# The gated sum of the expert results in the edge pass: 16 multiply-adds, or one product and three additions

## The chip, the cores and the metric

The kernel runs on one core of one Trainium2 chip. It is one program over five engines: TensorE (PE, with PEld for its weight loads), VectorE (DVE), ScalarE (ACT), GpSimd (POOL) and SyncE (SP). The metric is the time of one execution in microseconds on the device; of three runs the median is given. What a measurement of this kernel can tell from no change is about 0.2%, some 6 us.

## The reference, cut to what matters

Four layers run one after the other on 128 graphs of 128 nodes with 128 features each: a graph attention, a mixture of 8 experts, a second graph attention, and last a layer that gates 4 experts by an attention over 524288 edges. Only the last is touched:

```
h = x @ W_gat                                   # 16 columns: 4 heads x 4 experts
e = leaky_relu(a_src[src] + a_dst[dst]);  alpha = softmax of e over the edges of a node
agg = segment_sum(h[src] * alpha, dst) + b_gat
scores = layernorm(agg).reshape(M, 4, 4).mean(1)          # one score for each expert
topk_s, topk_i = top_k(scores, 2);  w = softmax(topk_s)
for ei in range(4):
    g = where(topk_i == ei, w, 0).sum(-1)                 # gate of expert ei, 0 for two of the four
    out = out + g * (gelu(x @ W1[ei] + b1[ei]) @ W2[ei] + b2[ei])
return x + out
```

The change is in the last sum: the gates times the results of the four experts, added to x.

## The kernel before

The first three layers and a sort of the edges by target fill the first part of the span. The edge pass (`edges_and_experts1`) is the rest. It has 32 turns, each for a unit of 4 graphs (`UNIT`), so for 4 x 128 nodes; x lies in SBUF as 128 nodes x 128 graphs x 128 features in float32 for the whole kernel. Each engine runs its own loop over the turns, and the order within an engine is the order of the code. No scheduler moves anything. The engines meet only at semaphores.

Turns are counted from 0 here. Turns 0 to 30 are of the first loop (L1495), turn 31 of the second (L1497). GpSimd's gathers of an iteration stand ahead of the window reads of the same turn, so gathers go on beside VectorE's turns 0 to 29, and none are left in turns 30 and 31.

GpSimd, per loop turn (L1532 to L1539): 16 gathers into buffer 0, a wait for buffer 1 (`rows_out[1]`), 16 gathers into buffer 1, a wait for buffer 0 and for `win_free`, and two window reads (`windows`, L1524). A gather (L1518) fetches 128 rows of the node table by the 128 indices in a column of `edge_ids`. So GpSimd issues 34 indirect transfers per turn. SyncE (L1558 to L1571) writes each filled buffer to the edge table; for the second it first waits for `win_seen`, which VectorE gives at the start of its turn (L1389).

VectorE, per turn (`turn`, L1371): it waits for the windows (`win_in`), scores and hides the edges (L1391 to L1410), gives the scores to ScalarE for the exponential (`scored`, `exped`), multiplies the messages (L1417) and sums them (L1426), updates the running sums, normalises (L1437 to L1452), and ranks the experts (L1456 to L1468), with one exponential on ScalarE between (`gap_s` at L1460, `gap_exped` at L1464). The gates are the tile `one`, called gates in the rows, 128 x 4 graphs x 4 experts. Then it waits for TensorE's results (`res_mm`, L1470), which stand in four banks of PSUM (`b_res`, expert by expert, 4 graphs x 128 features each), and combines them (L1474 to L1482), called the combine below. It ends with `summed` (ScalarE then sends y to memory), `res_free` (TensorE may write the results of the next unit), and with three loads of planned numbers into registers before the next turn (L1496).

TensorE, per turn (`turn`, L1637): four transposes, 8 products of 512 columns with ScalarE's Gelu behind each, then for each expert one product that sets the bias (L1650) and 8 of 128 columns (L1653). ScalarE makes the input of the transposes for the next unit only when it has done `gap_s` of this one, so TensorE starts the next unit behind L1460 of this turn and ends it some time in the next turn.

The order around the combine is written out by hand. `step` lets an instruction raise the counter `step_s`; `settle` waits until all of them have; `then` is both. The combine is 16 `scalar_tensor_tensor` of 128 elements per partition, four for each expert, one for each graph, since the gate of a node is one number per partition, graph and expert:

```
to = b_res[:, e, v, :] * one[:, v, e:e + 1] + so_far
```

`so_far` is x for the first expert and `weighed` (SBUF) after it; the last four write y, and a `settle` stands between the experts. Each has one operand in PSUM and one in SBUF.

Of the kernel before, what the change touches and what calls it, by code (L numbers as in the profile page):

```python
# [6 lines left out]
ALU = mybir.AluOpType  # L7
# [7 lines left out]
P = 128  # L15
# [37 lines left out]
UNIT = 4  # L53
# [12 lines left out]
HC1 = HIDDEN1 // P  # L66
# [1095 lines left out]
def edges_and_experts1(nc, sem, a, x, rstd, shift, node, found, counted, source_ids, row_id, table_dram, edges_dram, out, ident, ones):  # L1162
# [5 lines left out]
    E = TOP_EXPERTS  # L1168
    SPAN = UNIT * NODES
    ROOT_GUESS = float(0x5F3759DF)  # L1170
    with ExitStack() as ctx:
        def sb(name, shape, dt=F32):
            return ctx.enter_context(nc.sbuf_tensor(name, shape, dt))

        def ps(name, shape):
            return ctx.enter_context(nc.psum_tensor(name, shape, F32))
# [25 lines left out]
        s4, one, rank, w_taken = (sb(n, [P, UNIT, E]) for n in ("s4", "gates", "rank", "w_taken"))  # L1202
# [3 lines left out]
        w1, b1 = sb("x1_w1", [P, E, HIDDEN1]), sb("x1_b1", [P, E * HC1])  # L1206
        w2, b2 = sb("x1_w2", [P, E * HC1, FEAT]), sb("x1_b2", [P, E, FEAT])
        feat, featT = sb("x1_feat", [P, UNIT, FEAT]), sb("x1_featT", [P, SPAN])
        hid, weighed, y = sb("x1_hid", [P, E * HC1, SPAN]), sb("x1_weighed", [P, UNIT, FEAT]), sb("x1_y", [P, UNIT, FEAT])

        b_next, b_featT, b_hid, b_res = ps("b_next", [P, 512]), ps("x1_b_featT", [P, UNIT, P]), ps("x1_b_hid", [P, 2, SPAN]), ps("x1_b_res", [P, E, UNIT, FEAT])
        b_most, b_due, b_plan = b_featT[:, 0, :], b_hid[:, 0, 0:UNITS], b_res[:, 0, :, :]
# [8 lines left out]
        normed, turned, featT_s, hid_mm, hid_s, hid_free, res_mm, res_free, summed, out_done = (sem(f"x1_{n}") for n in (  # L1221
            "normed", "turned", "featT", "hid_mm", "hid", "hid_free", "res_mm", "res_free", "summed", "out_done"))
# [18 lines left out]
        def take(engine, semaphore, count):  # L1241
            engine.wait_ge(semaphore, count)
            engine.sem_inc(semaphore, -count)  # L1243
# [4 lines left out]
        def _(dve):  # L1248
# [76 lines left out]
            to = node[:, :, ROW:TAB]  # L1325
# [45 lines left out]
            def turn(came, unit, theirs, after):  # L1371
                mine, pair, after = bass.ds(unit * UNIT, UNIT), bass.ds(unit * PAIRS, PAIRS), bass.ds(after * PAIRS, PAIRS)
# [4 lines left out]
                def step(ins):  # L1377
                    ins.then_inc(step_s, 1)
                    done[0] += 1

                def settle():
                    dve.wait_ge(step_s, done[0])

                def then(ins):
                    step(ins)
                    settle()
# [84 lines left out]
                dve.sem_inc(hid_free, 1)  # L1471

                settle()
                for e in range(E):  # L1474
                    if e == E - 1:
                        take(dve, out_done, 16)
                    for v in range(UNIT):
                        so_far = x[:, bass.ds(unit * UNIT + v, 1), :].rearrange("p o f -> p (o f)") if e == 0 else weighed[:, v, :]
                        to = y[:, v, :] if e == E - 1 else weighed[:, v, :]
                        last = dve.scalar_tensor_tensor(to, b_res[:, e, v, :], one[:, v, e:e + 1], so_far, ALU.mult, ALU.add)  # L1480
                        step(last)
                    settle()  # L1482
                dve.sem_inc(summed, 1)
                dve.sem_inc(res_free, 1)
                take(dve, step_s, done[0])
# [9 lines left out]
            with dve.Fori(0, more) as t:  # L1495
                turn(lambda: dve.wait_ge(win_in, (t + 1) * (16 * PAIRS)), planned_unit(dve, t + 1), planned_left(dve, t + 1), planned_unit(dve, t + 2))  # L1496
            with dve.Fori(0, late) as m:  # L1497
                unit = (m + UNITS - rest) & (UNITS - 1)
                turn(late_came, unit, unit, (m + UNITS + 1 - rest) & (UNITS - 1))
# [165 lines left out]
def build(nc, a, out):  # L1665
# [6 lines left out]
    with ExitStack() as top:  # L1672
# [33 lines left out]
        with ExitStack() as ctx:  # L1706
# [48 lines left out]
            def _(dve):  # L1755
# [25 lines left out]
              keys_dram, slots_dram, rows_dram, edges_dram, ids_dram, table_dram)  # L1781
        renew_semaphores()
        edges_and_experts1(nc, sem, a, x, rstd, shift, tab, found, counted[:, :], ids_dram, row_id[:, :], table_dram, edges_dram, out, ident[:, :], ones)


# [52 lines left out]
```

## Time and profile before

| What | us |
|---|---|
| Median of 3 runs | 3113.96 |
| Lowest and highest of the 3 | 3112.32, 3117.3 |
| Span of the profiled execution | 3601.8 |
| Profiled span less the median | 487.8 |
| VectorE busy in it | 2257.8 |
| TensorE busy | 1935.1 |
| GpSimd busy | 1857.5 |
| ScalarE busy | 1215.1 |

The profiled execution is one execution taken by the hardware profiler; its own time is shown by the span from the first to the last instruction, and nothing else of it is listed. The times of the runs are without the profiler. Here the two are far apart, by 487.8 us, so durations of single instructions can be read from the profile, while the sum of its waits isn't that of a timed run. The shares of busy time are means over stages: the edge pass is about the last 1715 us of the span, and turn 0 starts at 1887.1.

### The profile page before, as it was taken

What the parts mean: (1) busy time and instruction counts of PE and PEld (TensorE: products, weight loads), DVE (VectorE), ACT (ScalarE), POOL (GpSimd) and SP (SyncE); (2) the same over time, 40 slices, a digit from 0 to 9 for tenths busy, and PEclk for the clock granted to TensorE, in tenths of its full rate; (3) what the DMA queues carried; (4) which work ended last, traced back from release to release, by engine and by line L of the source; (5) the groups of instructions that cost most, each with busy time, mean ns of one, the idle gap of its engine ahead of it and who ended that gap; (6) DMA issues with size and microseconds to landing.
All of it is one profiled execution on the core that took longest, in us unless ns stands there. A gap on an engine that the chain in (4) does not pass through costs nothing. (4 is left out here: it accounts for less than half of the span.)

```text
span 3601.8 us, 31245 instructions
## 1 busy us (share of the span) xinstructions
PE 1935.1 (54%) x8829; PEld 1316.8 (37%) x8829; DVE 2257.8 (63%) x4422; ACT 1215.1 (34%) x2447; POOL 1857.5 (52%) x1723
## 2 busy tenths in 40 slices
PE   1776642387878645567432455454544444454555
PEld 1555542255655434456311222232222222222223
DVE  8999886989999965554223454454553444544547
ACT  2676754244444323455311122122212122121222
POOL 5400248554544444445575656655655656656561
PEclk9998865699999867777555676676776677767768
DMA  5792001011111121101111111111111111111111
GB/s 198 250 391 84 16 23 39 24 40 37 46 44 41 36 60 40 56 20 23 42 27 23 32 33 32 32 28 38 32 33 32 32 28 31 38 28 32 37 29 30
DMA packets 170130, 192.35 MB, mean 53 GB/s; under 512 B 59241, under 2 KB 126096, under 8 KB 169008
## 3 DMA queue, kind: packets, MB, share of 16 engines
q1 hardware_dynamic: 107616, 118.69, 9.9%
q0 software_dynamic: 57088, 62.48, 8.4%
q10 hardware_dynamic: 5328, 9.97, 0.7%
q8 instruction: 49, 0.80, 0.1%
q14 instruction: 49, 0.40, 0.0%
HBM read 91.70 MB, written 105.25 MB: 55 GB/s over the span
## 5 line engine op out<-in xcount | busy, mean ns | idle before, releaser
L1518 POOL DMA_INDIRECT edge_rows<-node_table,edge_ids x1024 | 1006.5, 983 | 646.2 <-POOLq L1243 345.9
L1646 PE MATMUL x_b_hid<-x_featT,x_w 128*128 128x512 f32 x512 | 362.3, 854 | 281.4 <-PEq L1243 93.5
L1146 POOL DMA_INDIRECT token_results<-arena,token_of x160 | 251.1, 1569 | 294.3 <-ACT arena L1082 216.9
L583 DVE TENSOR_TENSOR sort_ping<-sort_pong 128x1024 f32<-128x1024 f32 (+1 forms) x232 | 395.1, 1744 | 11.3 <-issue 3.8
L1158 POOL DMA_INDIRECT arena<-keys,row_ids x256 | 249.3, 974 | 288.6 <-DVE counts L821 181.0
L583 DVE TENSOR_TENSOR sort_pong<-sort_ping 128x1024 f32<-128x1024 f32 (+1 forms) x230 | 389.9, 1736 | 8.7 <-ACT sort_ping L1016 3.7
L1139 POOL DMA_INDIRECT slots<-arena,send x128 | 177.8, 1389 | 371.9 <-ACT arena L1038 336.9
L1640 PE MATMUL x_b_featT<-ident,x_feat 128*128 128x128 f32 x128 | 34.8, 428 | 581.0 <-issue 385.3
L1653 PEld LDWEIGHTS x_b_res<-x_w,x_hid 128*128 128x128 f32 x2048 | 276.1, 216 | 152.1 <-issue 152.1
L1653 PE MATMUL x_b_res<-x_w,x_hid 128*128 128x128 f32 x2048 | 303.9, 307 | 39.8 <-issue 39.8
L1646 PEld LDWEIGHTS x_b_hid<-x_featT,x_w 128*128 128x128 f32 x512 | 118.9, 262 | 500.2 <-issue 300.9
L1600 ACT ACTIVATE x_hid<-x_b_hid,x_b 128x512 f32<-128x512 f32 x256 | 174.8, 687 | 294.9 <-DMA keys<-sort_pong 129.3
L90 ACT ACTIVATE arena<-x,shift,rstd 128x128 f32<-128x128 f32 x512 | 210.1, 486 | 98.8 <-DMA slots<-arena,send 87.5
L1640 PEld LDWEIGHTS x_b_featT<-ident,x_feat 128*128 128x128 f32 x128 | 22.9, 217 | 587.7 <-issue 587.7
L1607 ACT ACTIVATE w_taken<-w_taken 128x16 f32<-128x16 f32 x32 | 6.9, 216 | 586.5 <-ACTq L1243 357.3
L252 PE MATMUL banks<-arena 128*128 128x129 f32 x512 | 96.4, 347 | 183.3 <-DVE x L279 94.3
L1480 DVE SCALAR_TENSOR_TENSOR x_weighed<-x_b_res,gates,x_weighed 128x128 f32<-128x128 f32 x256 | 72.1, 344 | 193.9 <-DMA adjacent<-in_adj_dram 158.6
L1650 PE MATMUL x_b_res<-x_b,ones 1*128 1x512 f32 x256 | 162.9, 718 | 30.8 <-PEq L1243 27.0
L977 PEld LDWEIGHTS banks<-arena 128*128 128x128 f32 x1280 | 145.9, 192 | 30.3 <-issue 30.3
L252 PEld LDWEIGHTS banks<-arena 128*128 128x128 f32 x512 | 83.9, 248 | 194.1 <-issue 180.0
L977 PE MATMUL banks<-arena 128*128 128x128 f32 x1280 | 153.5, 278 | 0.0
L968 PE MATMUL banks<-arena 128*128 128x512 f32 x320 | 148.5, 608 | 1.8 <-issue 1.8
(346 smaller groups left out, 4059.0 us busy)
## 6 DMA issues: line engine op xcount, KB each, us to landing
edge_table<-zeros SPq DMA_DIRECT2D x8, 5120.0 KB, 35.7
edge_rows<-node_table,edge_ids POOLq DMA_INDIRECT x1024
arena<-slots SPq DMA_DIRECT2D x40, 260.0 KB
slots<-zeros SPq DMA_DIRECT2D x2, 5120.0 KB, 24.4
edge_table<-edge_rows SPq DMA_DIRECT2D x64, 160.0 KB
out_dram<-x_y ACTq DMA_DIRECT2D x33, 256.0 KB
x<-in_x_dram SPq DMA_DIRECT2D x4, 2048.0 KB, 20.2
adjacent<-in_adj_dram SPq DMA_DIRECT2D x32, 256.0 KB, 2.7
```

What stands on the lines that cost most here:

```text
L90: last = act.activation(out[:, u, :], x[:, bass.ds(b, 1), :].rearrange("p o f -> p (o f)"), ACT.Identity, bias=shift[:, bass.ds(b, 1)], sc ...
L252: last = pe.matmul(self.b_near[:, v, 0:FEAT + 1], self.probsT[:, v, :], self.right[:, n % self.deep, v, self.near], start=True, stop=True)
L583: step(dve.tensor_tensor(vb[:, :, t, :], va[:, :, 0, :], va[:, :, 1, :], op))
L977: last = pe.matmul(b_res[:, n % 2, r, :], hid[:, n % 2, c, r * P:(r + 1) * P], w2[:, e % 2, c, :], start=False, stop=(r == PER - 1 and c = ...
L1139: pool.indirect_dma_start(slots_dram, bass.IndirectOffsetOnAxis(send[:, q:q + 1], 0), sent_feat[:, n % 2, v, :], None, bounds_check=EXPERT ...
L1146: pool.indirect_dma_start(rows_dram, bass.IndirectOffsetOnAxis(token_of[:, n % 4, r:r + 1], 0), res[:, n % 2, r, :], None, bounds_check=TO ...
L1158: pool.indirect_dma_start(fetched[:, n % FETCHED, c, :], None, keys_dram, bass.IndirectOffsetOnAxis(row_ids[:, q:q + 1], 0)).then_inc(fetc ...
L1518: pool.indirect_dma_start(rows[:, u, c, :], None, table_dram, bass.IndirectOffsetOnAxis(ids[:, u, c:c + 1], 0)).then_inc(rows_in[u], 16)
L1600: act.activation(hid[:, c, :], b_hid[:, c % 2, :], ACT.Gelu, bias=b1[:, c:c + 1]).then_inc(hid_s, 1)
L1646: pe.matmul(b_hid[:, c % 2, :], w1[:, c // HC1, c % HC1 * P:(c % HC1 + 1) * P], featT[:, :], start=True, stop=True).then_inc(hid_mm, 1)
L1650: pe.matmul(b_res[:, e, :, :], ones[0:1, :], b2[0:1, e, :].unsqueeze(1).to_broadcast([1, UNIT, FEAT]), start=True, stop=False)
L1653: last = pe.matmul(b_res[:, e, v, :], hid[:, e * HC1 + c, v * P:(v + 1) * P], w2[:, e * HC1 + c, :], start=False, stop=(v == UNIT - 1 and ...
```

## The change

The tile `weighed` grows from 4 x 128 to 4 x 4 x 128 elements per partition. The 16 instructions become four, each over the whole unit: a product of all results with the gates (2048 elements, the gates repeated along the features by an access pattern), the sum of experts 0, 1 with 2, 3 (1024), the sum of the two halves (512), and the addition of x into y (512). Each waits for the one ahead of it. The wait for `out_done`, by which y is free, stands ahead of the last instruction, where it stood ahead of the last four.

```diff
-        hid, weighed, y = sb("x1_hid", [P, E * HC1, SPAN]), sb("x1_weighed", [P, UNIT, FEAT]), sb("x1_y", [P, UNIT, FEAT])
+        hid, weighed, y = sb("x1_hid", [P, E * HC1, SPAN]), sb("x1_weighed", [P, E, UNIT, FEAT]), sb("x1_y", [P, UNIT, FEAT])
@@
                 settle()
-                for e in range(E):
-                    if e == E - 1:
-                        take(dve, out_done, 16)
-                    for v in range(UNIT):
-                        so_far = x[:, bass.ds(unit * UNIT + v, 1), :].rearrange("p o f -> p (o f)") if e == 0 else weighed[:, v, :]
-                        to = y[:, v, :] if e == E - 1 else weighed[:, v, :]
-                        last = dve.scalar_tensor_tensor(to, b_res[:, e, v, :], one[:, v, e:e + 1], so_far, ALU.mult, ALU.add)
-                        step(last)
-                    settle()
+                then(dve.tensor_tensor(weighed[:, :, :, :], b_res[:, :, :, :], one[:, :, :].rearrange("p v e -> p e v").unsqueeze(3).to_broadcast([P, E, UNIT, FEAT]),
+                                       ALU.mult))
+                then(dve.tensor_tensor(weighed[:, 0:2, :, :], weighed[:, 0:2, :, :], weighed[:, 2:4, :, :], ALU.add))
+                then(dve.tensor_tensor(weighed[:, 0, :, :], weighed[:, 0, :, :], weighed[:, 1, :, :], ALU.add))
+                take(dve, out_done, 16)
+                then(dve.tensor_tensor(y[:, :, :], weighed[:, 0, :, :], x[:, mine, :], ALU.add))
                 dve.sem_inc(summed, 1)
                 dve.sem_inc(res_free, 1)
```

On VectorE, at the end of a loop turn, these instructions stood before (x_weighed, x_b_res and x_y are the tiles `weighed`, `b_res` and y; ISA rows are register work):

```order
L1468 TENSOR_TENSOR gates<-gates,gat_first 128x16
L1480 ISA
L1480 SCALAR_TENSOR_TENSOR x_weighed<-x_b_res,gates,x 128x128
...
L1480 SCALAR_TENSOR_TENSOR x_weighed<-x_b_res,gates,x_weighed 128x128 x8
L1480 SCALAR_TENSOR_TENSOR x_y<-x_b_res,gates,x_weighed 128x128 x4
L1495 REGISTER_ALU
```

And there, on the same engine at the same place, the changed kernel has:

```order
L1468 TENSOR_TENSOR gates<-gates,gat_first 128x16
L1474 TENSOR_TENSOR x_weighed<-x_b_res,gates 128x2048
L1476 TENSOR_TENSOR x_weighed<-x_weighed 128x1024
L1477 TENSOR_TENSOR x_weighed<-x_weighed 128x512
L1479 ISA
L1479 TENSOR_TENSOR x_y<-x_weighed,x 128x512
L1492 REGISTER_ALU
```

Sixteen rows of work and four of register work became four and one; nothing ahead of L1468 or behind the combine moved, and no other engine's order changed. Of the new four, the first reads PSUM and SBUF, the other three read two tensors in SBUF.

## Rows read from the trace of the kernel before

**Rows 1.** The page: span, and each engine's busy time and share

```profile
span 3601.8 us, 31245 instructions
...
PE 1935.1 (54%) x8829; PEld 1316.8 (37%) x8829; DVE 2257.8 (63%) x4422; ACT 1215.1 (34%) x2447; POOL 1857.5 (52%) x1723
```

**Rows 2.** Windows, turns 0 to 28: stretch, us, busy of each engine, PEclk, DMA, GB/s

```profile
1887.10:3499.10 1612.00, 754.81 (x2595) 407.10 (x2596) 752.75 (x2147) 334.71 (x519) 977.44 (x999) 0.68 0.15 32
```

**Rows 3.** Timeline of VectorE, turn 9: start us, length us, what, [idle before]

```profile
2405.84 0.89 DVE L1391 TENSOR_TENSOR win_score<-win,masked 128x320 f32<-128x320 f32 x2 [3.21 <-issue]
...
2432.31 1.13 DVE L1480 SCALAR_TENSOR_TENSOR x_weighed<-x_b_res,gates,x 128x128 f32<-128x128 f32 x4 [1.11 <-DVE gates L1468]
...
2448.41 1.13 DVE L1480 SCALAR_TENSOR_TENSOR x_y<-x_b_res,gates,x_weighed 128x128 f32<-128x128 f32 x4 [4.61 <-DMA adjacent<-in_adj_dram]
2457.05 0.89 DVE L1391 TENSOR_TENSOR win_score<-win,masked 128x320 f32<-128x320 f32 x2 [7.51 <-issue]
```

**Rows 4.** Timeline of VectorE, turns 29 to 31

```profile
3528.57 1.13 DVE L1480 SCALAR_TENSOR_TENSOR x_weighed<-x_b_res,gates,x 128x128 f32<-128x128 f32 x4 [0.16 <-DVE gates L1468]
...
3532.20 1.12 DVE L1480 SCALAR_TENSOR_TENSOR x_y<-x_b_res,gates,x_weighed 128x128 f32<-128x128 f32 x4 [0.18 <-DVEq L1243]
3536.54 0.89 DVE L1391 TENSOR_TENSOR win_score<-win,masked 128x320 f32<-128x320 f32 x2 [3.22 <-issue]
...
3567.88 0.89 DVE L1391 TENSOR_TENSOR win_score<-win,masked 128x320 f32<-128x320 f32 x2 [1.23 <-DVEq L1243]
```

**Rows 5.** Timeline of GpSimd, turn 9: behind its pauses, and beside the combine

```profile
2408.53 1.21 POOL L1518 DMA_INDIRECT edge_rows<-node_table,edge_ids  x1 [12.05 <-POOLq L1243]
...
2432.22 0.95 POOL L1518 DMA_INDIRECT edge_rows<-node_table,edge_ids  x1 [0.30 <-issue]
...
2459.75 1.21 POOL L1518 DMA_INDIRECT edge_rows<-node_table,edge_ids  x1 [7.81 <-POOLq L1243]
```

**Rows 6.** Timeline of GpSimd, window reads of two turns, an unbroken stretch

```profile
1881.11 0.95 POOL L1524 DMA_INDIRECT win<-edge_table,win_ids  x1 [0.30 <-issue]
...
1924.56 0.94 POOL L1524 DMA_INDIRECT win<-edge_table,win_ids  x1 [0.30 <-issue]
```

**Rows 7.** Timeline, turn 29 to 30: last step before ScalarE, first products, last matmul

```profile
3523.92 0.17 DVE L1460 TENSOR_TENSOR w_taken<-s,gat_first 128x16 f32<-128x16 f32 x1 [0.99 <-DVE gat_first L1458]
...
3531.55 5.75 PE L1646 MATMUL x_b_hid<-x_featT,x_w 128*128 128x512 f32 x9 [0.88 <-PEq L1243]
...
3551.67 2.05 PE L1653 MATMUL x_b_res<-x_w,x_hid 128*128 128x128 f32 x16
```

**Rows 8.** Groups by form, VectorE: busy us, mean ns of one | idle before

```profile
L583 DVE TENSOR_TENSOR sort_ping<-sort_pong 128x2048 f32<-128x2048 f32 x112 | 253.0, 2300 | 1.7
...
L583 DVE TENSOR_TENSOR sort_ping<-sort_pong 128x1024 f32<-128x1024 f32 x120 | 142.1, 1225 | 9.6 <-issue 3.8 <-ACT sort_pong L1016 2.8
...
L308 DVE TENSOR_TENSOR x<-x,arena 128x512 f32<-128x512 f32 x32 | 22.1, 692 | 1.1
L296 DVE TENSOR_TENSOR arena<-banks,bias 128x512 f32<-128x512 f32 x32 | 22.1, 691 | 106.6 <-remote 52.0 <-PE banks L264 39.1 <-issue 15.4
```

**Rows 9.** Timeline, gathers beside additions and products of 2048 elements

```profile
1818.01 2.29 DVE L1348 TENSOR_TENSOR acc<-masked,self_w 128x2048 f32<-128x2048 f32 x1
...
1819.10 2.02 POOL L1518 DMA_INDIRECT edge_rows<-node_table,edge_ids  x1 [0.31 <-issue]
...
1820.34 2.29 DVE L1350 TENSOR_TENSOR wide<-last_node,clamp_w 128x2048 f32<-128x2048 f32 x1
```

**Rows 10.** Timeline, gathers beside L1417 in turn 9

```profile
2414.26 2.89 DVE L1417 TENSOR_TENSOR win_msg<-win,win_score 128x1280 f32<-128x1280 f32 x2 [2.40 <-DVEq L1243]
...
2415.28 1.29 POOL L1518 DMA_INDIRECT edge_rows<-node_table,edge_ids  x1 [0.30 <-issue]
2416.87 1.09 POOL L1518 DMA_INDIRECT edge_rows<-node_table,edge_ids  x1 [0.30 <-issue]
```

**Rows 11.** Record of the gathers' line: duration ns min/median/max

```profile
L1518 POOL DMA_INDIRECT edge_rows<-node_table,edge_ids x1024: 941/947/2234, 1796.2 to 3521.5; - x171
```

## The prediction

> **What bounds the kernel now.** I read the page first. Span 3601.8 us, VectorE busy 63% and no engine near full [rows 1]; the span lies 487.8 us above the median of the runs, 3113.96. So the waits of this profile are not those of a timed run, and the question is which of them stay. The change is in the edge pass, so all else is read there.
>
> The windows view of turns 0 to 28 gives 1612 us for 29 turns, 55.6 us each, with VectorE busy for 753 and GpSimd for 977 [rows 2]. The timeline of VectorE shows why a turn is so long. In turn 9 the combine starts at 2432.31 and its last four end at 2449.53: 17.2 us, of which 3 x 1.13 and 1.12 are work, the rest idle between groups that wait for nothing but their own forerunner; the next turn starts at 2457.05, so the turn took 51.2 us [rows 3]. In turn 29, at whose end the gathers are over, the same 16 instructions take from 3528.57 to 3533.32, 4.75 us [rows 4]. The idle stretches are thus no cost of the instructions. They come while GpSimd issues gathers without a break, and the timed runs are 488 us shorter, so I take them as all but absent there.
>
> Without them VectorE needs: turn 30, 3536.54 to 3567.88, is 31.34 us; it has 1.23 us idle at the end where a turn followed by one of the first loop has 3.22, so 33.3 us per turn [rows 4].
>
> GpSimd needs more. In a stretch in which it never waits, the window reads of two turns start at 1881.11 and 1924.56: 43.45 us for 34 transfers, 1.25 each with 0.30 between [rows 6]; the median gather is 947 ns, the shortest 941 [rows 11]. In turn 9 it waited 12.05 us and behind it 7.81 [rows 5], because VectorE's late start of a turn holds back the write of the second buffer; with VectorE at 33 us these waits go.
>
> TensorE with ScalarE: from L1460 of turn 29 at 3523.92 to the last matmul at 3553.72 are 29.8 us [rows 7]. Of these, 22.2 lie behind the start of the first product at 3531.55. The granted clock was 0.68 of full over turns 0 to 28 [rows 2], so between its two levels, 2.4 and 1.2 GHz; were all of the 22.2 at the lower, they would be 44.4 and the whole 52. The loop goes L1460, matmuls, combine, next L1460 in two turns: (52 + 31.3)/2 = 41.7 us at the very worst, the 31.3 being 33.3 less the 2 us between L1460 and the combine.
>
> So 43.45 (GpSimd) stands above 41.7 and above 33.3. A check by the median: at 43.45 the 29 turns are 1260 us, 352 less than profiled; the other 136 of the 488 would lie in earlier stages. At 33.3 they would be 966, 646 less, more than the whole difference. If all the 488 were in these turns a turn would be 38.8. VectorE alone isn't the bound by either account.
>
> **What the change removes and adds on VectorE.** Removed: 4.75 us per turn [rows 4]. Added: a product of 2048 elements, a sum of 1024, two of 512. Rows of that size: 2.30, 1.225 and 0.69 us [rows 8]. That the product reads PSUM is priced by two additions of 512, 0.691 with a PSUM operand and 0.692 without [rows 8]: nothing. For gates read by a stride of zero I take nothing too, with 0.1 as the upper end (L1417, also with a repeated operand, takes 2.89 us for 2 x 1280 elements, 1.13 ns per element as against 1.12 [rows 8, 10]). Sum: 2.30 + 1.225 + 0.69 + 0.69 = 4.91, two gaps of 0.04 between dependent instructions (L1348 ends at 1818.01 + 2.29 = 1820.30, L1350 starts at 1820.34 [rows 9]), and 0.18 for the wait for y, as before [rows 4]: 5.16 us. So the combine is 0.4 us longer, with bounds 0.2 and 0.6. It reads and writes 4096 elements where it had 2048; what is saved is the start of 12 instructions. The register rows that go stood behind the wait at L1470 and beside L1468 (0.16 us idle ahead of the combine [rows 4]); at most 0.1 comes back. `res_free` and `summed` come 0.4 later; TensorE wants the first only behind its 8 products, and ScalarE the second behind its 8 Gelus, so nobody waits.
>
> The Trainium skill ("VectorE: DVE Perf Modes", section "Rules for kernel authors") says of chained operations: minimize the op count. By that alone 12 instructions less would be a gain; here each of the 16 costs (4.75/16) 0.30 us for 128 elements, 0.13 of it the elements, so 12 starts are worth 2 us and 2048 more elements cost 2.1, and the rule's gain is used up.
>
> If VectorE had 0.4 us more per turn and nothing else changed, then, with GpSimd the bound and 10 us of slack in every turn, turns 0 to 29 would stay and only turns 30 and 31 and the end of turn 29 would be longer: 3 x 0.4 = 1.2 us.
>
> **What it does to GpSimd.** A cost lies off VectorE. Gathers beside VectorE instructions of two SBUF tensors are longer: the one at 1819.10 took 2.02 us and ended at 1821.12, that is 0.82 behind the end of L1348 [rows 9]. With 0.95 alone [rows 11], such a gather stands still from 0.13 us behind its start until the VectorE instruction has ended. The same rule gives turn 9: L1417 is two instructions from 2414.26 to 2417.15; the gather at 2415.28 is 0.34 longer, that at 2416.87 0.14 [rows 10]. The old combine has one SBUF operand beside PSUM; the gather at 2432.22 ran beside its first four and took 0.95 [rows 3, 5]. So the old 16 cost GpSimd nothing, and the new product should not either, but the three sums, 1.225 + 0.69 + 0.69, should. One gather comes every 1.25 us. If one falls into the sum of 1024, it waits for its end, 0 to 1.1 us; the next comes 1.25 behind that, into the last sum (0.9 to 1.6 behind), and waits about 0.35. If none falls there, only 0.2 to 0.35 is left. Bounds: 0 (all slip through) and 1.5 us per turn. I take 0.7, the middle. With GpSimd the bound it adds in turns 0 to 29: 30 x 0.7 = 21 us.
>
> The Trainium skill ("SBUF — State Buffer", section "Who interferes with whom") says that a VectorE instruction with two SBUF inputs contends with a GpSimd instruction that reads SBUF, and that the second to issue waits for the whole of the first. By that rule the change is charged as here; the trace agrees, with 2.02 us for 0.95.
>
> **Sum.** 21 + 1.2 = 22 us, so 3114 + 22 = 3136. Against the profiled execution the sum is made otherwise: there the new combine has 4 instructions to be held up in place of 16, its 17.2 us may fall to 8, and the span may fall by up to 30 x 9 = 270 us though timed runs get longer.
>
> **Rivals.**
> (a) VectorE, or the loop of TensorE and VectorE, is the bound in timed runs. For it: 38.8 us, the mean if all the 488 is in the loop, is near the 41.7; against it, GpSimd's steady 1.25, which would have to be faster untraced. Price: 32 x 0.4 = 13 us if VectorE alone bounds, half of it with the two-turn loop: 3120 to 3127.
> (b) No change. Gathers slip past the sums, or the earlier pair L1417 shifts the gathers so that only the last sum is met, at 0.15 us or less: 30 x 0.1 + 1 = 4 us, 3118. For it: start times within a turn are the same every turn, so the meeting is the same 30 times over, and may be a lucky one.
> (c) Faster. The idle stretches of [rows 3] are in part in timed runs too. Place: between the groups of the combine. They cost 17.2 - 4.75 = 12.5 us of turn 9, of 17.9 idle in all (51.2 - 33.3). If timed turns are 38.8 us, of which 5.5 idle in that way, the combine's share is 3.8; with a quarter of the instructions some 2.9 of it go, less 0.4: 30 x 2.5 = 75 us, 3039. It decides from 0.6 us of idle per combine on, where the saving passes 0.4. Against it: GpSimd's 43.45 would still stand above.
>
> **How the numbers follow.** GpSimd bound and held up by at least 0.2 us a turn, my forecast: 0.53. (a) 0.15, (b) 0.22, (c) 0.10. The likeliest is 3136. The range: low end 3112, which leaves out (c) alone; high end 3152, from 30 x 1.2 and 1.2; its own range is 3121 to 3152. No change means within 0.2%, 6.2 us, of 3114, what a measurement of this kernel can tell. Faster: 0.10. Same: (b) and half of (a) with 0.22 + 0.07 = 0.29, less a little of (b) that ends above 3120: 0.27. Slower: 0.63.
>
> **What would show it.** In the profile of the changed kernel: four instructions of 2.3, 1.23, 0.69 and 0.69 us at the combine, 5.1 to 5.2 us in turns 30 and 31; gathers of 1.3 us to 2 beside them, and a mean gather above today's 0.98; shorter pauses of GpSimd behind L1518 as the profiled turn falls toward 45 us. I am wrong if the sums beside gathers leave them at 0.95, if timed runs are over 6 us faster (then the idle stretches are real), or if the product takes far over 2.3 us.

## The result, and the profile after

| | median us | lowest to highest | ratio to before | 95% interval |
|---|---|---|---|---|
| before | 3116.28 | 3112.32 to 3121.79 | | |
| changed | 3126.52 | 3125.52 to 3131.59 | 1.0039 | 1.0028 to 1.0049 |

Six runs each. The changed kernel is slower, by 0.0039 x 3116 = 12 us (the interval is 9 to 15, and the two medians differ by 10). The forecast was 3136, slower, with 3112 to 3152 for the time; the direction and the mechanism hold, the size is about half of the 22 us.

The page of the changed kernel:

```profile
span 3129.3 us, 30765 instructions
...
PE 1788.7 (57%) x8829; PEld 1235.4 (39%) x8829; DVE 2265.7 (72%) x4038; ACT 1204.6 (38%) x2447; POOL 1860.4 (59%) x1723
```

It answers to [rows 1] of before, and the first thing to see is that the span is 3129.3 us, not 488 above the timed runs but 3 from their median. (The profiled execution is the slowest of the six, 3131.59.) The long idle stretches are gone, and so this profile can be read as a whole. A second profile of the kernel before, told below, has a span of 3113.3 us. It is the one to compare with.

The window of turns 0 to 29 (columns as in [rows 2]):

```profile
1751.90:3062.70 1310.80, 688.35 (x2708) 381.50 (x2708) 787.05 (x1861) 340.92 (x540) 996.80 (x1017) 0.74 0.21 40
```

GpSimd's waits in these turns (what waited, for what: us in total, times, longest):

```profile
POOL edge_rows L1515 <- issue: 269.7, 885, 0.3
POOL edge_rows L1515 <- POOLq L1243: 21.9, 72, 0.3
POOL win L1521 <- issue: 18.3, 60, 0.3
```

1310.8 us for 30 turns are 43.69 each. No wait of GpSimd is over 0.3 us, the distance between any two of its transfers; the pauses of 12.05 and 7.81 us in [rows 5] are gone. VectorE waits instead, for the windows that GpSimd reads (its largest wait in the same turns):

```profile
DVE win_score L1391 <- DMA win<-edge_table,win_ids: 443.3, 30, 61.0
```

443.3 us in 30 waits: one of 61 at the start, the others some 13 us per turn. GpSimd is the bound, VectorE is not.

The combine of turn 9, which answers to [rows 3], with the gathers beside it (start us, length us, what, idle before; `...` stands for rows left out, here and below):

```profile
2170.24 2.29 DVE L1474 TENSOR_TENSOR x_weighed<-x_b_res,gates 128x2048 f32<-128x2048 f32 x1
...
2172.45 0.94 POOL L1515 DMA_INDIRECT edge_rows<-node_table,edge_ids  x1 [0.30 <-issue]
2172.56 1.23 DVE L1476 TENSOR_TENSOR x_weighed<-x_weighed 128x1024 f32<-128x1024 f32 x1
...
2173.70 0.95 POOL L1515 DMA_INDIRECT edge_rows<-node_table,edge_ids  x1 [0.30 <-issue]
2173.82 0.69 DVE L1477 TENSOR_TENSOR x_weighed<-x_weighed 128x512 f32<-128x512 f32 x1
...
2174.78 0.69 DVE L1479 TENSOR_TENSOR x_y<-x_weighed,x 128x512 f32<-128x512 f32 x1 [0.27 <-DVEq L1243]
2174.95 1.33 POOL L1515 DMA_INDIRECT edge_rows<-node_table,edge_ids  x1 [0.30 <-issue]
```

Four instructions, 2.29, 1.23, 0.69 and 0.69 us, 5.23 us from 2170.24 to 2175.47, where the 16 took 4.75 [rows 4]. The gather at 2172.45 took 0.94 and that at 2173.70 0.95, though each ran beside a sum of two SBUF tensors for nearly all its length: each had started 0.11 or 0.12 us ahead of the sum. The gather at 2174.95 started 0.17 us into the last addition and took 1.33; it ended 0.81 us behind the end of that addition. So the three sums meet three gathers, and only the last holds one up. It is so in all of turns 0 to 29: the gathers beside the first two sums start 0.10 to 0.14 us ahead of them and take 0.94 to 0.95, those beside the last addition start 0.15 to 0.18 behind its start and take 1.33 to 1.36.

Why is it so in every turn? The gathers beside L1417, which answer to [rows 10]:

```profile
2153.39 2.89 DVE L1417 TENSOR_TENSOR win_msg<-win,win_score 128x1280 f32<-128x1280 f32 x2 [2.40 <-DVEq L1243]
2154.47 1.23 POOL L1515 DMA_INDIRECT edge_rows<-node_table,edge_ids  x1 [0.30 <-issue]
2156.00 1.09 POOL L1515 DMA_INDIRECT edge_rows<-node_table,edge_ids  x1 [0.31 <-issue]
...
2157.40 0.97 POOL L1515 DMA_INDIRECT edge_rows<-node_table,edge_ids  x1 [0.30 <-issue]
```

L1417 ends at 2156.28, and the gather beside it ends at 2157.09, 0.81 later, the distance seen above. From there gathers come every 1.25 us, and the combine starts 13.96 us behind the end of L1417 on VectorE. In all 30 turns these two distances are 0.81 to 0.83 and 13.94 to 13.96 us, with 11 gathers begun between the end of L1417 and the combine. Both engines start from the same instant, which explains why the meeting is the same each time; no run takes this common start away, so that part is read from the rows and not tested.

### The profile page after: what moved, and what is told of

It reads as the page before. It is cut to its first block and busy times, and to the rows that moved or that the text cites. A ratio compares the mean times of both kernels' runs of the same rounds, so it can differ in the third digit from the quotient of the medians.

```text
span 3129.3 us, 30765 instructions
## 1 busy us (share of the span) xinstructions
PE 1788.7 (57%) x8829; PEld 1235.4 (39%) x8829; DVE 2265.7 (72%) x4038; ACT 1204.6 (38%) x2447; POOL 1860.4 (59%) x1723
## 5 line engine op out<-in xcount | busy, mean ns | idle before, releaser
L1391 DVE TENSOR_TENSOR win_score<-win,masked 128x320 f32<-128x320 f32 x64 | 28.7, 489 | 457.1 <-DMA win<-edge_table,win_ids 455.8
L1643 PE MATMUL x_b_hid<-x_featT,x_w 128*128 128x512 f32 x512 | 310.3, 759 | 28.3 <-PEq L1243 28.3
L1650 PEld LDWEIGHTS x_b_res<-x_w,x_hid 128*128 128x128 f32 x2048 | 245.8, 197 | 97.3 <-issue 97.3
L1650 PE MATMUL x_b_res<-x_w,x_hid 128*128 128x128 f32 x2048 | 270.9, 287 | 0.0
L1643 PEld LDWEIGHTS x_b_hid<-x_featT,x_w 128*128 128x128 f32 x512 | 107.2, 238 | 217.7 <-ACT x_hid L1597 126.6
L252 PE MATMUL banks<-arena 128*128 128x129 f32 x512 | 87.5, 324 | 134.4 <-DVE x L279 71.6
L1647 PE MATMUL x_b_res<-x_b,ones 1*128 1x512 f32 x256 | 143.8, 641 | 27.8 <-PEq L1243 27.8
L977 PEld LDWEIGHTS banks<-arena 128*128 128x128 f32 x1280 | 145.9, 192 | 30.3 <-issue 30.3
L1417 DVE TENSOR_TENSOR win_msg<-win,win_score 128x1280 f32<-128x1280 f32 x64 | 92.7, 1489 | 78.1 <-DVEq L1243 78.1
```

The lines of the kernel that those rows point to most:

```text
L977: last = pe.matmul(b_res[:, n % 2, r, :], hid[:, n % 2, c, r * P:(r + 1) * P], w2[:, e % 2, c, :], start=False, stop=(r == PER - 1 and c = ...
L1417: step(dve.tensor_tensor(msg[:, of_mate, :, :].rearrange("p t k (h e) -> p (t k) h e", h=HEADS), w_flat[:, :, 0:GAT].rearrange("p k (h e) ...
L1643: pe.matmul(b_hid[:, c % 2, :], w1[:, c // HC1, c % HC1 * P:(c % HC1 + 1) * P], featT[:, :], start=True, stop=True).then_inc(hid_mm, 1)
L1647: pe.matmul(b_res[:, e, :, :], ones[0:1, :], b2[0:1, e, :].unsqueeze(1).to_broadcast([1, UNIT, FEAT]), start=True, stop=False)
L1650: last = pe.matmul(b_res[:, e, v, :], hid[:, e * HC1 + c, v * P:(v + 1) * P], w2[:, e * HC1 + c, :], start=False, stop=(v == UNIT - 1 and ...
```

## The experiments

Each kernel ran against the kernel before on the same chip, and what it adds is told against that. The medians of before were 3115.7 to 3116.3 us in all of them.

**The kernel before once more, for a second profile.**

> The kernel before once more, for a second profile. In its first, 488 us longer than the timed runs, all engines but GpSimd stood still for stretches of each turn. If these belong to that one profiled execution, the span is near 3115 us now and VectorE's turns are 43.2 us long with no idle time inside the combine; if every profile of this kernel has them, and the fewer instructions of the changed one spare it, the span is near 3600 again.

Nothing was edited. The single time was 3115.69 us, and the page begins:

```profile
span 3113.3 us, 31205 instructions
...
PE 1784.0 (57%) x8789; PEld 1235.2 (40%) x8829; DVE 2253.6 (72%) x4422; ACT 1204.1 (39%) x2447; POOL 1843.0 (59%) x1723
```

So the 488 us of idle time belong to the one profiled execution, not to the kernel and not to profiling it. The first product L1417 and the combine of turn 9, now undisturbed:

```profile
2149.53 0.94 POOL L1518 DMA_INDIRECT edge_rows<-node_table,edge_ids  x1 [0.30 <-issue]
2149.54 2.91 DVE L1417 TENSOR_TENSOR win_msg<-win,win_score 128x1280 f32<-128x1280 f32 x2 [2.39 <-DVEq L1243]
...
2166.52 1.13 DVE L1480 SCALAR_TENSOR_TENSOR x_weighed<-x_b_res,gates,x 128x128 f32<-128x128 f32 x4 [0.16 <-DVE gates L1468]
...
2167.36 0.94 POOL L1518 DMA_INDIRECT edge_rows<-node_table,edge_ids  x1 [0.30 <-issue]
2167.68 2.29 DVE L1480 SCALAR_TENSOR_TENSOR x_weighed<-x_b_res,gates,x_weighed 128x128 f32<-128x128 f32 x8
...
2170.14 1.13 DVE L1480 SCALAR_TENSOR_TENSOR x_y<-x_b_res,gates,x_weighed 128x128 f32<-128x128 f32 x4 [0.17 <-DVEq L1243]
```

2166.52 to 2171.27 is 4.75 us, as in [rows 4]; in [rows 3] it was 17.2. The gather at 2149.53 started 0.01 us ahead of L1417 and took 0.94. Turns 0 to 29 take from 1750.6 to 3047.3 us, 43.22 each. The changed kernel's start at 1751.9 and take 43.69: 30 x 0.47 = 14 of the 16 us between the two spans lie there, 1.3 ahead of turn 0 and 0.6 in turns 30 and 31. Of the 14, 12.0 are the waits at the last addition; the other 2 lie in gathers beside L1391 to L1417, which come to 20 to 23 us in every trace of this case with L1417 as it was. What stopped the engines in the first execution is open.

**One more gather per buffer: is GpSimd the bound?**

> The kernel before with one more gather per buffer, a repeat of its first into rows that nobody reads: 36 indirect transfers a turn in place of 34, 64 more in all. Theory, GpSimd is the bound of turns 0 to 29: 64 x 1.25 = 80 us more, less the two or so that lie beside other work, ratio 1.025. Rival, VectorE or TensorE is the bound at 40 us or more: at most a third of it, ratio 1.008.

The main lines of the edit (left out: the buffer grows by one tile, and SyncE waits for 17 gathers and writes 16 tiles as before):

```diff
-                for c in range(PART_TILES):
+                for c in range(PART_TILES + 1):
...
-                                            bass.IndirectOffsetOnAxis(ids[:, u, c:c + 1], 0)).then_inc(rows_in[u], 16)
+                                            bass.IndirectOffsetOnAxis(ids[:, u, c % PART_TILES:c % PART_TILES + 1], 0)).then_inc(rows_in[u], 16)
```

3203.51 us against 3115.7, ratio 1.0281 (1.0266 to 1.0296), 88 us. That is 1.37 us for each of 64 gathers, more than the bare 1.25: the turns 0 to 29 are 46.09 us long, 2.87 above 43.22 for two gathers. The 0.37 above 2 x 1.25 are longer gathers: over the 30 turns those beside L1391 to L1417 lose 11 us more than in the kernel before. The rival, at most a third of 80 us, is out.

**Two reductions ahead of the old combine: what is VectorE's time worth?**

> The kernel before with two reductions (512 and 1024 elements, 2.0 us together, one operand, in PSUM) ahead of the 16 multiply-adds. Theory, VectorE has 10 us of slack in each of turns 0 to 29: only the last two or three turns grow, 3 x 2.0 = 6 us, ratio 1.002. Rival, VectorE is the bound: 32 x 2.0 = 64 us, ratio 1.020. Rival, the loop of TensorE and VectorE: half of it, 1.010.

The result goes to `pad`, a new tile of one column that nobody reads:

```diff
+                then(dve.tensor_reduce(pad[:, :], b_res[:, 0:1, :, :].rearrange("p e v f -> p (e v f)"), AX_X, ALU.max))
+                then(dve.tensor_reduce(pad[:, :], b_res[:, 0:2, :, :].rearrange("p e v f -> p (e v f)"), AX_X, ALU.max))
                 for e in range(E):
```

3117.8 against 3116.0, ratio 1.0007 (0.9999 to 1.0016). Two microseconds more on VectorE in each of 32 turns, 64 in all, cost 2, not told from none; the interval reaches to 5. The gather beside the longer reduction in turn 9, started 0.11 us behind it, isn't held up:

```profile
2167.63 1.22 DVE L1475 TENSOR_REDUCE pad<-x_b_res 128x1 f32<-128x1024 f32 x1
2167.74 0.94 POOL L1520 DMA_INDIRECT edge_rows<-node_table,edge_ids  x1 [0.30 <-issue]
```

The expected 6 us counted turns 29, 30 and 31, and the two profiles show one turn's worth. Turn 29 has slack like those ahead of it. Turn 30 grows from 31.2 to 33.2 us, but turn 31 gives that back, since it waits for ScalarE's exponential ahead of L1417. In the second profile of the kernel before:

```profile
3089.07 2.89 DVE L1417 TENSOR_TENSOR win_msg<-win,win_score 128x1280 f32<-128x1280 f32 x2 [4.32 <-DVEq L1243]
```

And in this one:

```profile
3092.76 2.89 DVE L1417 TENSOR_TENSOR win_msg<-win,win_score 128x1280 f32<-128x1280 f32 x2 [2.40 <-DVEq L1243]
```

The wait shrinks from 4.32 to 2.40 us. From the start of turn 30 to the end are 66.0 us before and 68.1 here.

**The same length with one operand pair in SBUF.**

> The kernel before with a reduction of 512 elements and then an addition of two SBUF tensors of 1024 elements into an unused tile ahead of the 16 multiply-adds: as long on VectorE (2.0 us) as the reductions of 512 and 1024, but the second has two SBUF operands. Theory: the addition meets a gather in every turn and holds it up by about 0.8 us: 30 x 0.8 = 24 us, and 6 at the end, 30 us, ratio 1.010, against 1.002 for the two reductions. Rival, only VectorE's length counts: both kernels the same.

`idle` is a new tile that nobody reads:

```diff
+                then(dve.tensor_reduce(pad[:, :], b_res[:, 0:1, :, :].rearrange("p e v f -> p (e v f)"), AX_X, ALU.max))
+                then(dve.tensor_tensor(idle[:, :, :], x[:, 0:2 * UNIT, :], x[:, 2 * UNIT:4 * UNIT, :], ALU.add))
                 for e in range(E):
```

3148.58 against 3115.91, ratio 1.0117 (1.0101 to 1.0132): 36 us, or 33 by the medians, where the last kernel cost 2. Turn 9:

```profile
2173.36 0.69 DVE L1475 TENSOR_REDUCE pad<-x_b_res 128x1 f32<-128x512 f32 x1
...
2174.08 1.22 DVE L1476 TENSOR_TENSOR idle<-x 128x1024 f32<-128x1024 f32 x1
2174.32 1.80 POOL L1521 DMA_INDIRECT edge_rows<-node_table,edge_ids  x1 [0.30 <-issue]
```

The addition into `idle` runs from 2174.08 to 2175.30; the gather that started 0.24 behind it took 1.80 us and ended 0.82 behind its end. Summed over turns 0 to 29, gathers beside this addition are 25.8 us longer than 0.95 each. VectorE's length is the same in both kernels (6.85 us from the first reduction to the end of the combine); the operands of one instruction differ. With 2 us at the end that makes 28, as far as the profiled execution lies above the second one of before (3141.1 and 3113.3). It was the fastest of the four runs; the 5 to 8 us that the medians and the ratio show above 28 have no trace, and their cause is open.

**The changed combine without two SBUF operands.**

> The whole-unit combine with the same arithmetic, but no instruction of two SBUF tensors: experts 0 and 1 are multiplied in place in PSUM, 2 and 3 into SBUF, and each of the additions takes one operand from PSUM. Six instructions (2 x 1024, 4 x 512), about 5.4 us in place of 5.24. Theory, GpSimd bound and held up only by the sum that adds x (0.40 us a turn): the 12 us come back, the time is that of the kernel before plus 1 to 2 us (two turns at the end that VectorE bounds), ratio 1.000 to 1.001; gathers beside the combine take 0.95 us. Rival, the longer combine costs by itself: the time stays at or above that of the changed kernel, ratio 1.004 or more.

```diff
-                then(dve.tensor_tensor(weighed[:, :, :, :], b_res[:, :, :, :], one[:, :, :].rearrange("p v e -> p e v").unsqueeze(3).to_broadcast([P, E, UNIT, FEAT]),
-                                       ALU.mult))
...
+                gates_of = one[:, :, :].rearrange("p v e -> p e v").unsqueeze(3)
+                step(dve.tensor_tensor(b_res[:, 0:2, :, :], b_res[:, 0:2, :, :], gates_of[:, 0:2, :, :].to_broadcast([P, 2, UNIT, FEAT]), ALU.mult))
+                then(dve.tensor_tensor(weighed[:, 2:4, :, :], b_res[:, 2:4, :, :], gates_of[:, 2:4, :, :].to_broadcast([P, 2, UNIT, FEAT]), ALU.mult))
+                step(dve.tensor_tensor(b_res[:, 0, :, :], b_res[:, 0, :, :], weighed[:, 2, :, :], ALU.add))
+                then(dve.tensor_tensor(weighed[:, 1, :, :], b_res[:, 1, :, :], weighed[:, 3, :, :], ALU.add))
+                then(dve.tensor_tensor(b_res[:, 0, :, :], b_res[:, 0, :, :], weighed[:, 1, :, :], ALU.add))
                 take(dve, out_done, 16)
+                then(dve.tensor_tensor(y[:, :, :], b_res[:, 0, :, :], x[:, mine, :], ALU.add))
```

3115.78 against 3116.0, ratio 1.0001 (0.9991 to 1.0011). The last addition and its gather in turn 9:

```profile
2172.21 0.69 DVE L1481 TENSOR_TENSOR x_y<-x_b_res,x 128x512 f32<-128x512 f32 x1 [0.27 <-DVEq L1243]
2172.24 0.94 POOL L1517 DMA_INDIRECT edge_rows<-node_table,edge_ids  x1 [0.30 <-issue]
```

The combine is 5.37 us long, longer than the changed kernel's, and the time is that of before. The gathers stand elsewhere against its instructions than in the changed kernel (0.03 us into the last addition where it was 0.17), so this kernel alone doesn't tell the operands from the place. The next one does.

**Only the last addition with an operand in PSUM.**

> The changed kernel with its four instructions and their lengths kept; only the sum of 512 writes its result to PSUM, so that the last addition reads PSUM and x and has one SBUF operand. The sums of 1024 and 512 still read two SBUF tensors. Theory: in the changed kernel only the last addition meets a gather (0.40 us in each of 30 turns), the two others slip between gathers, so this one operand brings back all of the 12 us: ratio to before 1.000. Rival, all three sums cost a share: ratio 1.002 to 1.003. Rival, VectorE's length: 1.004.

```diff
-                then(dve.tensor_tensor(weighed[:, 0, :, :], weighed[:, 0, :, :], weighed[:, 1, :, :], ALU.add))
+                then(dve.tensor_tensor(b_res[:, 0, :, :], weighed[:, 0, :, :], weighed[:, 1, :, :], ALU.add))
                 take(dve, out_done, 16)
-                then(dve.tensor_tensor(y[:, :, :], weighed[:, 0, :, :], x[:, mine, :], ALU.add))
+                then(dve.tensor_tensor(y[:, :, :], b_res[:, 0, :, :], x[:, mine, :], ALU.add))
```

3117.72 against 3115.7, ratio 1.0006 (0.9997 to 1.0015). Turn 9:

```profile
2166.62 0.94 POOL L1515 DMA_INDIRECT edge_rows<-node_table,edge_ids  x1 [0.30 <-issue]
2166.74 1.23 DVE L1476 TENSOR_TENSOR x_weighed<-x_weighed 128x1024 f32<-128x1024 f32 x1
...
2167.87 0.95 POOL L1515 DMA_INDIRECT edge_rows<-node_table,edge_ids  x1 [0.30 <-issue]
2168.00 0.70 DVE L1477 TENSOR_TENSOR x_b_res<-x_weighed 128x512 f32<-128x512 f32 x1
...
2168.97 0.69 DVE L1479 TENSOR_TENSOR x_y<-x_b_res,x 128x512 f32<-128x512 f32 x1 [0.27 <-DVEq L1243]
2169.12 0.94 POOL L1515 DMA_INDIRECT edge_rows<-node_table,edge_ids  x1 [0.30 <-issue]
```

The instructions are those of the changed kernel in number and length. The gather at 2169.12 starts 0.15 us into the last addition (0.12 to 0.16 in all 30 turns), as the one at 2174.95 did there with 0.17, and takes 0.94 in place of 1.33. That one operand is worth 10 of the 12 us by the ratios, and the interval holds all of them.

**The changed combine later by 0.73 and by 1.27 us: does the place matter?**

> The changed kernel with one reduction of 512 elements (0.73 us with its gap, one operand, in PSUM) ahead of the product, so that the three sums come 0.73 us later. Theory: gathers stand 1.25 us apart at the same place in every turn, and a later start puts the sum of 1024 onto one of them, with a wait of about 0.7 more per turn: 30 x 0.7 = 21 us, and 2 at the end, so 23 us above the changed kernel, ratio to before 1.011. Rival, VectorE's length counts: 32 x 0.73 = 23 us too (told apart by the next kernel). Rival, nothing but the last turns: 2 us, ratio 1.0045.

> The same with a reduction of 1024 elements (1.27 us with its gap), one whole distance between gathers. Theory: the sums meet the gathers as in the changed kernel (0.40 us a turn), so in turns 0 to 29 nothing is lost; 3 x 1.27 = 4 us at the end; ratio to before 1.005, and faster than the kernel with the shorter reduction by some 19 us. Rival, VectorE's length counts: 32 x 1.27 = 41 us above the changed kernel, ratio 1.017, and slower than the one with the shorter reduction.

```diff
+                then(dve.tensor_reduce(pad[:, :], b_res[:, 0:1, :, :].rearrange("p e v f -> p (e v f)"), AX_X, ALU.max))
                 then(dve.tensor_tensor(weighed[:, :, :, :], b_res[:, :, :, :], one[:, :, :].rearrange("p v e -> p e v").unsqueeze(3).to_broadcast([P, E, UNIT, FEAT]),
```

(0:2 in place of 0:1 for the longer.) Both against 3116.0: the shorter delay 3150.69, ratio 1.0117 (1.01 to 1.0133), the longer 3128.46, ratio 1.0041 (1.0028 to 1.0054). More work is faster by 22 us. Turn 9 with the shorter delay:

```profile
2176.66 1.22 DVE L1477 TENSOR_TENSOR x_weighed<-x_weighed 128x1024 f32<-128x1024 f32 x1
...
2176.93 1.77 POOL L1516 DMA_INDIRECT edge_rows<-node_table,edge_ids  x1 [0.30 <-issue]
...
2178.87 0.69 DVE L1480 TENSOR_TENSOR x_y<-x_weighed,x 128x512 f32<-128x512 f32 x1 [0.27 <-DVEq L1243]
2179.01 1.38 POOL L1516 DMA_INDIRECT edge_rows<-node_table,edge_ids  x1 [0.30 <-issue]
```

The sum of 1024 now starts at 2176.66, 0.27 ahead of the gather at 2176.93, which takes 1.77 (in most turns 0.41 ahead, and 1.63); the gather behind it meets the last addition as before, 1.38. With the longer delay the sum of 1024 starts behind its gather again:

```profile
2174.66 0.94 POOL L1516 DMA_INDIRECT edge_rows<-node_table,edge_ids  x1 [0.30 <-issue]
2174.79 1.22 DVE L1477 TENSOR_TENSOR x_weighed<-x_weighed 128x1024 f32<-128x1024 f32 x1
...
2177.01 0.69 DVE L1480 TENSOR_TENSOR x_y<-x_weighed,x 128x512 f32<-128x512 f32 x1 [0.27 <-DVEq L1243]
2177.16 1.36 POOL L1516 DMA_INDIRECT edge_rows<-node_table,edge_ids  x1 [0.30 <-issue]
```

The gathers take 0.94 and 1.36. Over turns 0 to 29 the sum of 1024 holds gathers up by 20.6 us with the shorter delay and by 0.2 with the longer; the last addition by 13.0 and 12.2, and by 12.0 in the changed kernel.

**The same cure at another place: a version faster than both.**

> The kernel before (16 multiply-adds) with ScalarE's exponential of the scores written to PSUM, 320 elements for each mate, in two banks that are free at that time; the product L1417 then has one SBUF operand, and the sum of the weights (L1421) is two reductions. In the changed kernel L1417 holds up two gathers of every turn, by 0.44 us a turn together. Theory, port of two-SBUF instructions on a bound GpSimd: 30 x 0.44 = 13 us less than before, ratio 0.996, and gathers beside L1417 of 0.95 us. Rival, gathers aren't the bound, or what L1417 does to them is made up elsewhere: ratio 1.000.

(Left out: VectorE waits for three results of ScalarE where it waited for two.)

```diff
+        HALF_SC = PAIRS * WINDOW * HEADS
+        sc_exp = [b_next[:, 0:HALF_SC], b_featT[:, :, :].rearrange("p v i -> p (v i)")[:, 0:HALF_SC]]
...
-                                           sc[:, of_mate, :, :].rearrange("p t k h -> p (t k) h").unsqueeze(3).to_broadcast([P, PAIRS * WINDOW, HEADS, E]),
+                                           sc_exp[m].rearrange("p (k h) -> p k h", h=HEADS).unsqueeze(3).to_broadcast([P, PAIRS * WINDOW, HEADS, E]),
...
-                step(dve.tensor_reduce(sums[:, :, :], by_head, AX_X, ALU.add))
+                for m in range(MATES):
+                    step(dve.tensor_reduce(sums[:, m * PAIRS:(m + 1) * PAIRS, :], sc_exp[m].rearrange("p (t k h) -> p t h k", t=PAIRS, h=HEADS), AX_X, ALU.add))
...
-                act.activation(sc[:, :, :, :], sc[:, :, :, :], ACT.Exp).then_inc(exped, 1)
+                for m in range(MATES):
+                    act.activation(sc_exp[m], sc[:, m * PAIRS:(m + 1) * PAIRS, :, :].rearrange("p t k h -> p (t k h)"), ACT.Exp).then_inc(exped, 1)
```

3103.16 against 3115.91, ratio 0.9964 (0.995 to 0.9978), 11 us faster than before and 23 below the changed kernel's 3126.52. The product of the messages, L1417 before, in turn 9:

```profile
2142.13 1.49 DVE L1419 TENSOR_TENSOR win_msg<-win,b_next 128x1280 f32<-128x1280 f32 x1 [2.49 <-DVEq L1245]
2143.29 0.94 POOL L1521 DMA_INDIRECT edge_rows<-node_table,edge_ids  x1 [0.30 <-issue]
2143.54 1.48 DVE L1419 TENSOR_TENSOR win_msg<-win,x_b_featT 128x1280 f32<-128x1280 f32 x1
2144.54 0.94 POOL L1521 DMA_INDIRECT edge_rows<-node_table,edge_ids  x1 [0.30 <-issue]
```

It is as long as before, 1.49 and 1.48, and the gathers beside it take 0.94 where they took 1.23 and 1.09 in the changed kernel. The turns 0 to 29 are 42.90 us long, 0.33 less than before where 0.44 was expected. L1417 held gathers up by 12.8 us over 30 turns of the kernel before and does so no more, but 4 us of that come back at other instructions of the turn, most of them ahead of L1417, which now meet the gathers at other places.

## Why the prediction was right, point by point

- **The bound.** GpSimd's 43.45 us per turn, read from an unbroken stretch of a disturbed profile, is 43.22 in the undisturbed one. The account of the 488 us, 352 in turns 0 to 28 and 136 ahead, nearly holds: turn 0 starts at 1750.6 us in place of 1887.1, 136.5 earlier, and turns 0 to 28 are 359 us shorter (1252.5 for 1612.0). VectorE waits 391 us for windows in turns 0 to 29 of that profile, 13.0 for each of 30 turns, where a turn that waits for no gathers has 3.2 [rows 4]: the slack is 10 us. The worth of its time is shown by the two reductions (2 us for 64).
- **The combine's length.** 5.16 us forecast, 5.23 to 5.24 measured: 2.30, 1.225 and twice 0.69 were 2.29, 1.23 and twice 0.69. The product, with PSUM and repeated gates as operands, took 2.29 us for 2048 elements, as long as one with both operands in SBUF [rows 8]. The gap ahead of the last addition, with the register work, was 0.27 for 0.18. The term of 3 x 0.4 = 1.2 us for the last turns came out at half of that: from the start of turn 30 to the end are 66.7 us for 66.0, since turn 31 waits for ScalarE and gives back what turn 30 adds.
- **The operands.** That a gather begun during a VectorE instruction with two SBUF operands stands still until that instruction ends is shown in both directions: added in the old kernel (36 us as against 2), and taken from the new one (ratio 1.0001 and 1.0006). The 0.82 us from the end of the one to the end of the other is 0.81 to 0.83 in every row here. The Trainium skill ("SBUF — State Buffer", section "Who interferes with whom") has the rule that two SBUF inputs contend and one doesn't, and that the second to issue waits for the whole of the first. The traces agree on the operands, and on the wait where VectorE is first. They don't agree where the gather is first: the sum of 1024 started 0.11 us into a gather of 0.94, 0.03 behind the product's end, and took 1.23 us, the same gap and length as in turns 30 and 31, where no gather runs. Neither of the two waits then.
- **The size, the step that was off.** The term "30 x 0.7 = 21 us" was taken as the middle between 0 and 1.5 us per turn. It measured 0.40, the wait at the last addition alone, 12.0 us over 30 turns. The text had both parts, "about 0.35" for the last sum, and 0 to 1.1 us for the sum of 1024, and took a mean over the second as if the place were random. It isn't: in every turn the sum of 1024 starts 0.10 to 0.12 us behind the start of a gather and misses it. The rival (b) named this, "the earlier pair L1417 shifts the gathers so that only the last sum is met", and priced it at 0.15 us or less. The forecast was right in its mechanism, and (b) in the place; the true figure stands between the two. That the total came within 10 us of the forecast is in part luck: a combine 0.73 us later gave 3150.69, close to the upper end of 3152.
- **The other rivals.** (a), VectorE or the loop with TensorE as the bound, had the range 3120 to 3127, and the measured 3126.52 lies in it; the time alone doesn't decide against it. The two reductions do (2 us, where it would have cost 64 or 32), and so does the extra gather. (c), idle stretches in timed runs, is out by the second profile.
- **The profiled span.** "May fall by up to 270 us" had the cause wrong: it fell by 472 us, because this execution was undisturbed, and the second one of the kernel before fell by 488.
- **The signs named.** Four instructions of the forecast lengths were there, and one gather of 1.33 us a turn. The mean gather was to rise above 0.98; it is 0.984 us, but that of the undisturbed profile of before is 0.971, and 0.98 was the mean of the disturbed one. The sign of being wrong, sums that leave gathers at 0.95, came true for two of the three.

## What to carry to other kernels

Where GpSimd's indirect transfers are the bound, as here, VectorE's time in its slack is free, and its operands are not: a VectorE instruction with two tensors in SBUF holds up the gather that starts during it until it ends. One operand in PSUM, even if a result must be written there for it, cost nothing here (0.70 us for 0.69) and removed the wait. Before taking a mean for such a wait, ask what fixes the place of one engine's instructions against the other's in a loop. Here the same meeting came back in every turn: the same sums, 0.73 us later, cost 24 us more, and 1.27 us later nothing that could be measured.

## What the runs showed that was not expected

- One profiled execution of an unchanged kernel was 488 us longer than another (3601.8 and 3113.3 us), with VectorE, ScalarE and TensorE standing idle between instructions, for up to 5 us at a time inside the combine. VectorE's instructions were as long in both. A span far above the timed runs is a reason to take a second profile before any wait of the first is read.
- More added work was faster than less: with 1.27 us more per turn the changed kernel was 13 us above before, with 0.73 us more 36.
- A gather that starts ahead of a VectorE instruction with two SBUF operands isn't held up by it, even if it is ahead by only 0.01 us (0.94 us beside L1417 above). At these products and sums, one that starts 0.11 us or more behind is held up in every trace, until the instruction ends. No gather of these runs starts between 0.01 and 0.11 us behind.
